# A post-norm decoder layer on one core: another order for filling the pipeline, pad rows written piece by piece during attention, eight places for row tiles, and 71 of them

## What is computed

```
x = norm(x + (linear_attention(x) + x))              # rotary, l2-normed q and k, W_in, W_out
x = norm(x + cross_attention(image=ctx, latents=x))  # 16 heads of 64, 128 keys each
x = norm(x + moe(x))                                 # 8 experts, best 2, 128 -> 512 -> 128, exact gelu
```

## Time and profile before

| | us |
|---|---|
| median of three runs | 1544.98 |
| lowest and highest of them | 1544.03, 1548.81 |
| the profiled execution | 1550.83 |
| its span, first to last instruction | 1548.9 |
| TensorE busy (matmul records) | 1376.8 (89%) |
| VectorE, ScalarE, GpSimd busy | 1135.8 (73%), 1149.7 (74%), 902.6 (58%) |
| mean granted TensorE clock | 0.961 of full |

### The profile page before, as it was taken

How to read it: one execution, slowest core, us unless ns; L and a number is a source line. 1 busy time by engine, 2 the same in 40 slices (tenths; PEclk the granted TensorE clock), 3 DMA queues, 4 the chain that set the end, 5 groups by cost and what they waited for, 6 DMA issues and landing times. The chain is left out here.

```text
span 1548.9 us, 37505 instructions
## 1 busy us (share of the span) xinstructions
PE 1376.8 (89%) x10765; PEld 1290.8 (83%) x10765; DVE 1135.8 (73%) x4170; ACT 1149.7 (74%) x4085; POOL 902.6 (58%) x1233
## 2 busy tenths in 40 slices
PE   6799999999999999999999999999994799999940
PEld 4699899898998899989999899998983798898830
DVE  4467777777777777777777777777665687787765
ACT  3588888888888888888888888888872455555535
POOL 4455666666666666666666666666544255555565
PEclk8899999999999999999999999999997799999975
DMA  3000000000000000000000000000003776777746
GB/s 91 11 11 11 17 15 17 19 15 17 15 17 19 15 17 15 17 19 15 17 15 17 19 15 17 15 17 8 10 10 59 219 238 210 220 227 219 218 148 192
DMA packets 64629, 96.24 MB, mean 62 GB/s; under 512 B 10892, under 2 KB 48786, under 8 KB 64306
## 3 DMA queue, kind: packets, MB, share of 16 engines
q1 hardware_dynamic: 44738, 71.90, 15.7%
q0 software_dynamic: 8896, 16.94, 3.2%
q10 hardware_dynamic: 10800, 5.06, 1.2%
HBM read 71.55 MB, written 23.35 MB: 61 GB/s over the span
## 5 line engine op out<-in xcount | busy, mean ns | idle before, releaser
L698 ACT ACTIVATE probs<-ps_s,neg_max 128x128 f32<-128x128 f32 x1024 | 361.7, 365 | 163.7 <-DVE neg_max L945 160.6
L513 POOL TENSOR_TENSOR probs_n<-probs,inv_sum 128x512 f32<-128x512 f32 x256 | 266.8, 1042 | 219.2 <-DVE inv_sum L951 211.7
L1367 PE MATMUL ps_s<-kvT,u_sb 128*128 128x128 f32 x2048 | 274.8, 277 | 0.8 <-issue 0.8
L1380 PE MATMUL ps_o<-value_w,tT 128*128 128x128 f32 x2048 | 260.2, 275 | 1.9 <-ACT tT L716 1.8
L1367 PEld LDWEIGHTS ps_s<-kvT,u_sb 128*128 128x128 f32 x2048 | 254.4, 191 | 7.0 <-issue 1.0
L1380 PEld LDWEIGHTS ps_o<-value_w,tT 128*128 128x128 f32 x2048 | 244.1, 192 | 2.9 <-ACT tT L716 2.9
L956 DVE TENSOR_TENSOR pT_lo<-ps_pT,pT_hi 128x512 fp32r<-128x512 f32 x256 | 175.5, 686 | 84.9 <-ACT pT_hi L707 84.9
L611 POOL DMA_INDIRECT y_rows<-wvT,f_id x144 | 145.1, 1008 | 154.7 <-DVE wvT L1284 100.2
L945 DVE TENSOR_REDUCE neg_max<-ps_s 128x4 f32<-128x512 f32 x256 | 176.9, 691 | 42.7 <-PE ps_s L1367 32.2
L698 ACT ACTIVATION_READ_ACCUMULATOR probs<-ps_s,neg_max 128x1 f32 x1024 | 207.4, 203 | 0.0
L1390 PE MATMUL ps_pT<-ident,probs_n 128*128 128x128 f32 x1024 | 157.7, 276 | 37.5 <-DVE pT_lo L956 36.6
(11 more groups left out here) (274 smaller groups left out, 3564.7 us busy)
## 6 DMA issues: line engine op xcount, KB each, us to landing
u_sb<-in_expert_w SPq DMA_DIRECT2D x45, 578.0 KB
tT<-in_expert_w SPq DMA_DIRECT2D x27, 578.0 KB
f_x<-x_rows SPq DMA_DIRECT2D x72, 130.0 KB
tT<-y_rows SPq DMA_DIRECT2D x16, 512.0 KB, 4.7
x_raw<-in_x SPq DMA_DIRECT2D x64, 64.0 KB, 1.8
c_raw<-in_ctx_in SPq DMA_DIRECT2D x64, 64.0 KB, 2.0
out<-u_sb ACTq DMA_DIRECT2D x16, 256.0 KB, 2.3
y_rows<-wvT,f_id POOLq DMA_INDIRECT x144
```

Source lines behind the costliest of these rows:

```text
L513: nc.gpsimd.tensor_tensor(probs_n[:, sl], probs[:, sl], inv_sum[:, sl, :].rearrange("p (u o) -> p u o", o=1).to_broadcast([P, UP, P]), ALU ...
L698: last = nc.scalar.activation(probs[:, sl, j], ps_s[sl][:, j * P:(j + 1) * P], ACT.Exp, bias=neg_max[:, sl, j:j + 1], accum_out=sums[:, sl ...
L1367: last = nc.tensor.matmul(ps_s[sl][:, j * P:(j + 1) * P], u_sb[:, c // 2, BT * p + b, h:h + 2].rearrange("p h s -> p (h s)"), kvT[:, c, 2 ...
L1380: last = nc.tensor.matmul(ps_o[:, 0:D], tT[:, (p + 1) % 2, h], value_w[:, h], start=(h == 0), stop=(h == H - 1))
```

## The change

- **Filling.** The order of the jobs is now in, W_q, W_k, the four "m" (5 to 8), then (EARLY = 9) W_v (9, 10) and the four "v" (11 to 14). Jobs 9 to 13 are done inside period 0 and 14 in period 1, in the banks `ps_o` and `ps_t`, each behind the copy of the one before; `out_part` of period 1 waits for the last two. The loads of W_k and W_v are two, W_v after tiles 2 and 3, and tile 1 is loaded ahead of W_q. All five hand-written lists of the filling are put in another order; VectorE's `stats(j)` waits for `c_hat` of two tiles earlier.
- **Pads.** The eight loads at the end, their addresses (`pad_f`, `pad_i`) and the wait for them are gone. SyncE's period t writes rows 128t to 128t+127 of all eight regions (1024 rows; 66 pieces, four in flight), and `route` waits for piece j ahead of tile j's scatter.
- **Rows.** `f_x` has eight places (X_SLOTS); a load waits for the tile eight back. NF is 71. Weights 1 and 2 go out behind the rows of tile 0.
- **Gelu.** ScalarE applies Gelu to one column of scratch after its last gate exponential.

```diff
-    most = (2 * tokens + experts * (FFN_ROWS - 1)) // FFN_ROWS
-    return -(-most // 8) * 8
+    return (2 * tokens + experts * (FFN_ROWS - 1)) // FFN_ROWS
...
+        jobs += turned_jobs(wq_raw, 0, wqT) + turned_jobs(wkv_raw, 0, wkT)
+        jobs += [("m", g, None) for g in range(4)]
+        EARLY = len(jobs)
+        jobs += turned_jobs(wkv_raw, H * HD, wvT)
+        jobs += [("v", g, heads_of(g, value_w[:])) for g in range(4)]
+        def job_bank(at):
+            if at < EARLY:
+                return banks[at % BANKS]
+            return ps_t if at == EARLY + 1 else ps_o
...
             load(0)
+            load(1)
             sp.dma_start(wq_raw[:], w_q).then_inc(s_wq, 16)
-            load(1)
-            sp.dma_start(wkv_raw[:], w_kv).then_inc(s_wkv, 16)
-            sp.dma_start(wo_raw[:], w_o.rearrange("(c p) n -> p c n", p=P)).then_inc(s_wo, 16)
+            sp.dma_start(wkv_raw[:, 0:H * HD], w_kv[:, 0:H * HD]).then_inc(s_wk, 16)
             load(2)
             load(3)
+            sp.dma_start(wkv_raw[:, H * HD:2 * H * HD], w_kv[:, H * HD:2 * H * HD]).then_inc(s_wv, 16)
+            sp.dma_start(wo_raw[:], w_o.rearrange("(c p) n -> p c n", p=P)).then_inc(s_wo, 16)
...
+            regions = x_rows[0:E * CAP, :].rearrange("(e r) d -> r e d", e=E)
+            def clear(n):
+                q = n % PAD_RING
+                sp.wait_ge(pad_filled[q], 16 * (n // PAD_RING))
+                sp.dma_start(regions[n * P:(n + 1) * P], pad_row[:].rearrange("p (o d) -> p o d", o=1).to_broadcast([P, E, ROW])
+                             ).then_inc(pad_filled[q], 16)
             def period(t, c):
                 if on(t, 6):
                     load(t + 6)
+                if t < CAP // P:
+                    clear(t)
...
-            sp.wait_ge(tab_ready, 1)
-            for e in range(E // 2):
-                at = sp.value_load(pad_i[0:1, e:e + 1], min_val=0, max_val=E * CAP - T)
-                sp.dma_start(x_rows[bass.ds(at, T), :].rearrange("(b p) d -> p b d", p=P), pad_rows).then_inc(pad_filled, 16)
...
-                sp.wait_ge(f_y_done, count(TB * i - TB * (RING - 1)))
+                sp.wait_ge(f_y_done, count(TB * i - TB * (X_SLOTS - 1)))
...
+                if isinstance(i, int) and i == 0:
+                    for n in range(1, AHEAD):
+                        weights(n, n)
...
-            sp.wait_ge(tab_ready, 2)
-            for i in range(AHEAD):
-                weights(i, i)
+            sp.wait_ge(tab_ready, 1)
+            weights(0, 0)
...
+                pool.wait_ge(pad_filled[j % PAD_RING], 16 * (j // PAD_RING + 1))
...
+            act.wait_ge(gexp_done, NT)
+            nc.scalar.activation(sq_junk[:, 0, 0:1], eps_ln[:, 0:1], ACT.Gelu)
...
             prepare(0)
             turn_x(0)
-            prepare(1)
+            turn_x(1)
             pe.wait_ge(win_kept, 1)
             make_qkv(0)
...
+            make_qkv(1)
+            prepare(1)
+            turn_queries(0)
             prepare(2)
...
             latents_part(0)
             turn_rows_back(0)
             latents_part(1)
-            project(3)
+            turn_queries(2)
             latents_part(2)
             turn_rows_back(1)
+            latents_part(3)
+            project(2)
+            turn_queries(3)
+            latents_part(4)
+            project(3)
             turn_x(4)
...
+                    if t == 0 and k == 0:
+                        prepare(EARLY)
+                        prepare(EARLY + 1)
+                    if t == 0 and k:
+                        prepare(EARLY + 1 + k)
+                    if t == 1 and k == 0:
+                        prepare(EARLY + 5)
```

More of the change, by code:

```diff
@@ L52, in decoder_layer @@
     ROW = D + 2
-    RING, W_RING = 4, 8
+    RING, W_RING, X_SLOTS = 4, 8, 8
     ZT = 4
@@ L284, in decoder_layer @@
         s_wq = sem("s_wq")
-        s_wkv = sem("s_wkv")
+        s_wk = sem("s_wk")
+        s_wv = sem("s_wv")
         s_wo = sem("s_wo")
@@ L314, in decoder_layer @@
         x_routed = [sem("x_routed0"), sem("x_routed1")]
-        pad_filled = sem("pad_filled")
-        f_in = [sem(f"f_in{q}") for q in range(RING)]
+        PAD_RING = 4
+        pad_filled = [sem(f"pad_filled{q}") for q in range(PAD_RING)]
+        dump_filled = sem("dump_filled")
+        f_in = [sem(f"f_in{q}") for q in range(X_SLOTS)]
         fw_in = [sem(f"fw_in{q}") for q in range(W_RING)]
@@ L747, in period @@
                         keep_rows(t + 2)
+                    if t == 0 and k != 2:
+                        keep_prepared((EARLY, EARLY + 2, None, EARLY + 4)[k])
             keep_prepared(0)
@@ L786, in _ @@
             periods(act, period)
-            act.wait_ge(tab_ready, 1)
-            act.wait_ge(pad_ready, 5)
-            for e in range(E // 2, E):
-                at = act.value_load(pad_i[0:1, e:e + 1], min_val=0, max_val=E * CAP - T)
-                act.dma_start(x_rows[bass.ds(at, T), :].rearrange("(b p) d -> p b d", p=P),
-                              pad_row[:].rearrange("p (o d) -> p o d", o=1).to_broadcast([P, TB, ROW])).then_inc(pad_filled, 16)
+            act.wait_ge(gexp_done, NT)
+            nc.scalar.activation(sq_junk[:, 0, 0:1], eps_ln[:, 0:1], ACT.Gelu)
             def upper_weights(i, q):
@@ L1112, in period @@
                     place_all()
+                if t == 0:
+                    keep_prepared(EARLY + 3)
                 if unit_on(t, 1):
@@ L1147, in stats @@
             def stats(j):
+                dve.wait_ge(c_hat_done, count(j - 1))
                 in_sums(j)
@@ L1371, in out_part @@
             def out_part(t, k, p):
+                if t == 1 and k == 1:
+                    pe.wait_ge(*prep_kept(len(jobs) - 2))
+                    pe.wait_ge(*prep_kept(len(jobs) - 1))
                 if k == 1:
@@ L1528, in _ @@
             project(0)
-            prepare(8)
+            prepare(3)
             project(1)
-            prepare(9)
+            prepare(4)
+            prepare(5)
+            turn_latents(0)
+            prepare(6)
+            turn_latents(1)
             turn_x(2)
+            prepare(7)
             make_qkv(2)
             turn_x(3)
-            prepare(10)
-            turn_latents(0)
-            prepare(11)
+            prepare(8)
             make_qkv(3)
-            turn_queries(2)
-            turn_latents(1)
-            prepare(12)
-            prepare(13)
-            project(2)
-            prepare(14)
-            turn_queries(3)
-            for kept in range(TURNED, len(jobs)):
+            for kept in range(5, EARLY):
                 pe.wait_ge(*prep_kept(kept))
```

157 lines of the change are left out of this document (72 added, 85 removed).

## The result

The changed kernel takes 1536.74 us (median of six runs, 1534.82 to 1541.03) against 1546.61 for the kernel before beside it (six runs, 1540.26 to 1549.77). The ratio is 0.9943, with a 95% interval from 0.9918 to 0.9969: 8.8 us faster, between 4.8 and 12.7. The forecast was 12.4 us, 1532.6 in a range from 1517 to 1543.

What follows compares the result with a forecast made beforehand. TensorE, nearly always busy, bounds the attention; filling, feed-forward start and feed-forward have idle time. Gains of 2.1 (filling), 4.8 (start) and 5.5 (feed-forward), pieces zero, sum to 12.4 us: 1544.98 to 1532.6, range 1517 to 1543.

Steps and rivals of the forecast that it cites:

- Filling: Start through periods 0 and 1: first scores 5.6 us earlier, less 3.5 paid in those periods, 2.1 us gained.
- I take 5.7, two thirds: First latents product to first scores: chains of tiles 2 and 3 cost between nothing and 8.6 us; 5.7 taken.
- Periods 0 and 1: First attention periods: six moved jobs bring 5.4 us of TensorE work, less 1.9 of room, costing 3.5.
- Pads in pieces: Attention: pad-row pieces of 532 KB, one per period, delay neither loads nor scatters; cost zero.
- Start of the feed-forward: Last count of rows to first tiles: first product 5.8 us earlier, 1.0 given back, 4.8 us gained.
- I give back 1.0: Second feed-forward tile: its rows, queued behind weights 1, 2 and 3, come hardly late; 1.0 us lost.
- Feed-forward: Feed-forward tiles: one tile of 72 less gains 3.9 us, eight places 1.6 of row waits; 5.5 us together.
- the filling only changes its waits: Filling: scores stay at 62.16 while periods 0 and 1 still pay 3.5 us; 1538.2 us, chance 0.16.
- the clock stays at 1.2 GHz: First latents product to first scores: interleaved work keeps TensorE at half clock, 4.7 us lost; 1537.3 us, chance 0.08.
- The pieces hold up nothing: Attention rival: scatters wait behind whole pieces, delaying VectorE's refill every period, 72 us over 60 periods; 1605 us, chance 0.05.
- The pad rows were what the rows waited for: Feed-forward start; rival denied this: scatters or weights land as late, so 4.8 us stay out; 1537.4 us, chance 0.05.
- the feed-forward would lose all of TensorE's idle time: Feed-forward: with rows early, TensorE's 18.0 us of idle time go, not 1.6; 1516.2 us, chance 0.08.

Runs made afterwards that it cites:

- the others: The unedited changed kernel measured again among the follow-up experiments against the kernel before: 1542.63 us against 1556.39, ratio 0.9919.
- the two runs alone: The kernel before with only 71 row tiles in place of 72: 1551.30 us, ratio 0.9965; with only eight places for row tiles: 1554.27 us, ratio 0.9990.

## Why the prediction was right, and where not

The time, the sign and the range hold: 8.8 us (4.8 to 12.7) in the first runs and 12.6 (8.4 to 16.7) in the others, against 12.4. The terms do so less well, and that their sum comes so near is in part luck: in the pair of traces the filling gave 3.8 us more than forecast, and the feed-forward 4.7 less; alone, the filling gave 4.4 more, the start of the feed-forward some 4 less.

**Filling, forecast 2.1, measured 5.9 in the pair of traces and 6.5 alone.** The step that was mis-sized is the chain from the first latents product to the first scores. "I take 5.7, two thirds" of two holes of 4.32; the two chains left one hole of 1.17, and the stretch grew from 12.8 to 16.3, by 3.5. Nor are holes what it grew by: TensorE is busy for 13.18 us of it where it was 10.05, and idle for 3.2 where it was 2.75. What the prediction counted as waiting was work moved there (turns and projections), part of it at a granted clock of 0.76 on average instead of 0.87. The first latents product came at 36.15 where I had 38. Of that, the working was off in its parts: the six jobs were given 9.5 us and the order 4.3, and the run with the jobs put back shows 6.5 (42.60 against 36.10 in the changed kernel's run beside it) and 6.7. That the price of a value product at half clock would go with the order, and not only with the product, was not seen: with the preparations in one run TensorE had its full speed back by 38 to 41 us, where by the durations of its products the kernel before had it at 52.8. Periods 0 and 1 paid 3.8 where I had 3.5.

**Pads in pieces, forecast 0, measured 0.** Neither the scatters nor the loads feel them, not even twice as many. The rule of the Trainium skill that was weighed there ("DMA: Bandwidth & Descriptors", Queues, rings and completion order) fits this: with 77 GB/s of pieces beside them the scatters cost the periods nothing. But no run here can tell turns by packets from turns by whole pieces, since a scatter that waited for a piece of 4.8 us would still land in time. VectorE waits for a landed scatter twice, both at the end of the attention, as before.

**Start of the feed-forward, forecast 4.8, alone nothing (between 3.3 lost and 2.5 gained, worked out from its interval).** The way to the first product was right, 5.8 forecast, 6.3 in the pair and 5.0 here. The step that failed is the second tile: "the second is nearer, as no pad rows are left to slow the engines, and I give back 1.0". The engines were not slowed, they were full: DMA share 0.97 at 337 GB/s, and rows behind three weight loads came 5.1 us after their issue. 2.5 us went back there (1.5 to 3.0 in other traces), and now and then as much again by the clock. With these rows loaded first the second product is back at 4.55 behind the first.

**Feed-forward, forecast 5.5, measured 7.3 in the medians of the two runs alone (5.1 and 2.2) and 0.85 in the pair of profiles.** The tile was worth its time; the places agree with the 1.6 that I gave them, in an interval (1.1 lost to 4.2 gained) that holds nothing too. The waits for rows did go, but TensorE then waited for VectorE instead, so "behind a wait that goes stand others" came true more fully than I took it. The pair of profiles alone would have called this step wrong; it compares one execution in which the beat was often broken with one in which it held.

**The rivals.** That the filling only changes its waits is out: first scores at 51.9 to 53.4 in all the kernels that have the changed filling whole. That the clock stays at 1.2 GHz in it is out as a whole and true in part: the products ran at half speed from 36.1 to about 40.5 and again from about 48 to 50.6, some 7 us of this stretch, where before it was some 3 (49.3 to about 52.5). I estimate from these times that it cost 1.9 of the 4.7 us that the rival was priced at. "Perfetto Trace Analysis" of the Trainium skill (Matmul Optimizations) was read against the change; the trace agrees with it in part, as the granted clock did fall once more, behind the holes of 1.17 and 1.70 that stand among the latents products. The pieces hold up nothing. The pad rows were what the rows waited for; but no run parts them from the new order of the first loads. Of the 6.2 us by which the first row load goes out earlier, I estimate from the earlier trace rows that two weight issues of 1.24 make up 2.5. The argument for it, that the DMA engines carry mostly pad rows there, was wrong: the eight loads of 130 KB are 1.06 of the 3.99 MB that move between 1188.1 and 1207.8. That the feed-forward would lose all of TensorE's idle time did not come about, for the reason that was given: rows were named for a fifth of it. Most of the rest goes with the place of the scatters, as the three kernels with held scatters show. The profile of before already had these long tiles, and I had not followed them.

**A version better than both.** The changed kernel with both scatters held back and the rows of tile 1 early: 1529.76 us, 0.9829 of before, 27 us below it and 13 below the changed kernel.

## What to carry to other kernels

When loads are put in a new order ahead of a stage, write down for each of the first tiles which loads stand ahead of its own on the queue: a wait that goes from tile 0 is easily found again at tile 1. Two profiles of a stage with a beat of unequal tiles do not tell what a change is worth there: look at the spread of the runs, and compare kernels with one part changed. And where the idle time of a busy engine recurs in every second tile, follow one such tile through all engines before giving it to the transfer that is named most often, and look for the tiles of the same trace that have the same overlap and no delay.

## What the runs showed of the hardware that was not expected

**A count that arrives late.** In the changed kernel TensorE's increment for the last result product reached an idle VectorE 0.04 us after the product's recorded end where no scatter issue of GpSimd lay across it, and mostly 0.9 to 1.0 us after it where a second issue had begun 0.24 us ahead of the product. ScalarE, waiting for the same count, got it at about the same time. It is the increment that is held, by the trace's own record of semaphores. In the tile that is shown above this count changes at 1267.03, and the next one of TensorE at 1267.11, 0.08 us apart, while their products end 0.72 apart; from 1266.32 to 1266.98 no semaphore of any engine or transfer changes.

An issue that lies across the product is not enough for it. In the tile after it, the first issue (1269.01 to 1270.04) lies across the end of the last product in the same way, and the count changes 0.01 us after that end, 1269.57. And two tiles with a second issue in the same place, the first of the changed kernel, the second of the kernel with eight places alone, show a count that is 0.24 and 0.04 late:

```profile
1448.83 1.95 PE L1625 MATMUL ps_t<-u_sb,wkv_raw 128*128 128x128 f32 x16
1450.27 0.97 POOL L630 DMA_INDIRECT y_rows<-wvT,f_id  x1 [0.31 <-issue]
1451.02 0.42 DVE L1289 TENSOR_TENSOR wqT<-ps_t,u_sb 128x256 f32<-128x256 f32 x1 [0.91 <-PE ps_t L1625]
```

```profile
1473.78 1.95 PE L1601 MATMUL ps_t<-tT,wkv_raw 128*128 128x128 f32 x16
1475.23 0.97 POOL L611 DMA_INDIRECT y_rows<-wvT,f_id  x1 [0.30 <-issue]
1475.77 0.42 DVE L1276 TENSOR_TENSOR wqT<-ps_t,tT 128x256 f32<-128x256 f32 x1 [0.70 <-PE ps_t L1601]
```

What else has to come together is open.

**A granted clock that the durations contradict.** The changed kernel's two profiled executions show the same stretch with the same work in the same time, once at a granted clock of 0.50 and once at 1.00; first the first execution, then the second:

```profile
20.00:36.00 16.00, 14.52 (x48) 10.39 (x48) 7.61 (x26) 6.94 (x18) 6.73 (x11) 0.50 0.06 16
```

```profile
20.00:36.00 16.00, 14.52 (x48) 10.38 (x48) 7.57 (x26) 6.94 (x18) 6.70 (x11) 1.00 0.06 15
```

The eight products of a W_q by W_k group last 2.07 us in both, and eight products of as many columns 1.06 in the attention. In the filling the durations are to be trusted, and the row of the granted clock only where it agrees with them. By the durations the lower level lasted until 38 to 41 us in both, and came back for some two microseconds between 46 and 51, where the record agrees in both.

**A dip of the clock in period 1.** Both kernels with the rows of tile 1 early show 19.2 us for period 1, at a granted clock of 0.91 on average, where the others with the new filling and its jobs in the periods have 17.6. The edit lies 1100 us later; why the clock fell there is open.
